# A Mamba-and-FFN sandwich block on one core: the chunk output computed turned, with the weights in the array and the decayed scores moving

## The reference, cut to what matters

```python
def step(state, inp):
    x_t, b_t, c_t, dt_t = inp
    decay = jnp.exp(dt_t * a)[..., None, None]
    b_bar = dt_t[..., None] * b_t
    state = decay * state + b_bar[..., None] * x_t[:, :, None, :]
    y_t = jnp.einsum('bhn,bhnp->bhp', c_t, state)
    return (state, y_t)
...
y = y + d_param[None, None, :, None] * xh
```

## Time and profile before

| | before |
|---|---|
| median of 3 runs | 1528.94 us (1528.52 to 1531.23) |
| the profiled execution: its time / its span | 1531.44 / 1529.7 us |
| PE (TensorE matmul) busy | 1426.4 us, 93% |
| PEld (weight loads) busy | 986.9 us, 65% |
| DVE (VectorE) / ACT (ScalarE) / POOL (GpSimd) busy | 1092.1 / 828.8 / 439.2 us |
| mean granted clock of TensorE | 0.974 |

### The profile page before, as it was taken

How to read it: one execution, slowest core, us unless ns; L and a number is a source line. 1 busy time by engine, 2 the same in 40 slices (tenths; PEclk the granted TensorE clock), 3 DMA queues, 4 the chain that set the end, 5 groups by cost and what they waited for, 6 DMA issues and landing times.

```text
span 1529.7 us, 28256 instructions
## 1 busy us (share of the span) xinstructions
PE 1426.4 (93%) x9712; PEld 986.9 (65%) x9712; DVE 1092.1 (71%) x2424; ACT 828.8 (54%) x1718; POOL 439.2 (29%) x487
## 2 busy tenths in 40 slices
PE   4999999998999989999999999999899999999776
PEld 3484758676485856758577675867658585675654
DVE  5454786858777686876859678685877769586665
ACT  3555574555745475553746447454674547555231
POOL 2020242214331232313422134321333134321343
PEclk8899999999999999999999999999999999999888
DMA  6000000101000010100001010010100000000000
GB/s 225 1 15 1 15 1 1 42 1 44 1 15 28 2 44 1 42 1 16 29 1 43 1 44 1 2 42 1 44 1 17 26 1 28 1 28 1 28 1 28
DMA packets 33351, 33.22 MB, mean 22 GB/s; under 512 B 4888, under 2 KB 31640, under 8 KB 33184
## 3 DMA queue, kind: packets, MB, share of 16 engines
q1 hardware_dynamic: 33184, 31.11, 6.2%
HBM read 22.72 MB, written 8.39 MB: 20 GB/s over the span
## 4 chain that ended last, share of the span: by engine, by line
PE 66%; issue 14%; DVE 10%; POOL 5%; ACT 2%; SPq 1%; DMA 0%; POOLq 0%; DVEq 0%; ACTq 0%
PE bank L1291 20%; PE bank L1473 7%; PE bank L1460 7%; PE bank L1377 6%; PE bank L1410 5%; PE bank L1445 4%; PE bank L1389 4%; PE bank L1369 3%; PE bank L1397 3%; PE bank L1359 2%; PE bank L1361 2%; SPq L548 1%; PE bank L1301 1%; DVE un L937 1%; POOL yT L670 1%
## 5 line engine op out<-in xcount | busy, mean ns | idle before, releaser
L686 POOL TENSOR_TENSOR xdw<-xdt,decays 128x512 f32<-128x512 f32 x64 | 66.7, 1043 | 430.3 <-DVE xdt L1043 408.1
L1291 PE MATMUL bank<-sh,WbT 128*128 128x512 f16 x768 | 174.3, 383 | 10.3 <-DVE sh L967 10.1
L1291 PE MATMUL bank<-sh,WcT 128*128 128x512 f16 x768 | 175.5, 379 | 0.0
L881 ACT ACTIVATE yk<-bank,decays 128x64 f32<-128x64 f32 x512 | 112.1, 330 | 86.4 <-PE bank L1389 86.4
L962 DVE SCALAR_TENSOR_TENSOR xs<-xi,taps,xs 128x512 f32<-128x512 f32 x192 | 152.5, 805 | 8.7 <-ACT xs L787 4.4
L1473 PE MATMUL bank<-sign2T,hh 128*128 128x256 f16 x1024 | 151.2, 275 | 2.0 <-DVE hh L1157 2.0
L868 ACT ACTIVATE mt<-bank 128x512 f32<-128x512 f32 x128 | 69.5, 596 | 148.3 <-PE bank L1361 148.3
L1410 PE MATMUL bank<-xdt,mt 128*128 128x64 f32 x1024 | 142.9, 262 | 0.0
L1291 PEld LDWEIGHTS bank<-sh,WbT 128*128 128x128 f16 x768 | 73.6, 98 | 100.6 <-issue 14.5
L1410 PEld LDWEIGHTS bank<-xdt,mt 128*128 128x128 f32 x1024 | 134.9, 192 | 2.2
L1291 PEld LDWEIGHTS bank<-sh,WcT 128*128 128x128 f16 x768 | 75.1, 98 | 87.1
(11 more groups left out here) (182 smaller groups left out, 2755.1 us busy)
## 6 DMA issues: line engine op xcount, KB each, us to landing
xt<-L_attn_input_tensor_dram SPq DMA_DIRECT2D x16, 512.0 KB, 4.8
u<-L_attn_input_tensor_dram SPq DMA_DIRECT2D x16, 512.0 KB, 3.7
out_dram<-u SPq DMA_DIRECT2D x16, 512.0 KB, 3.0
yT<-in_L_ffn_w_dram SPq DMA_DIRECT2D x2, 1024.0 KB, 14.1
zs<-in_L_attn_Wb_dram SPq DMA_DIRECT2D x1, 1024.0 KB, 8.6
zs<-in_L_attn_Wc_dram SPq DMA_DIRECT2D x1, 1024.0 KB, 10.8
BT<-in_L_attn_Wx_dram SPq DMA_DIRECT2D x1, 512.0 KB, 4.7
BT<-in_L_attn_Wz_dram SPq DMA_DIRECT2D x1, 512.0 KB, 6.1
```

Of the source, the lines that this page charges most:

```text
L686: pool.tensor_tensor(xdw[n % 2][:, :, :], xdt[n % 2][:, :, :], per_head(decays[:, 1, q, :]), ALU.mult)\
L881: last = nc.scalar.activation(yk[n % 2][:, h, :], bank(t, ("YI", j, q))[:, h * HD:(h + 1) * HD], ACT.Copy, scale=decays[:, 0, q, h:h + 1])
L1291: mm = nc.tensor.matmul(bank(t, key)[:, :], w[i][:, k, cols(m)], v[h][:, k, :], start=(a == 0), stop=(a == len(terms) - 1))
```

## The change

The output of a chunk is computed with channels on the partitions. `back` takes `xdt` (128 rows, 64 columns) as weights and moves `mt` (128 columns), and writes head h = 2c + g to partitions 64g to 64g + 63 and the columns of c. The part carried from the state goes into the same bank before it: `carry` takes the state as weights and moves `Cd`, which is C times the decay of each token. So Y needs neither yk nor a turn, and VectorE adds it to `yT` in one instruction. The step `turn` goes, with its keys and its place in all lists. YI is now the first part of Y, and a bank of Y is held from `carry` to the end of `back`.

`Cd` is new work: a product E in `front` (64 rows of fp16 weights, 512 columns moving), an Exp of 128x512 on ScalarE, and a multiplication of 128x512 by C on GpSimd. The decays lose their first third. `of_source` and `of_target` swap which of the two is kept by head group.

```diff
@@ PE front @@
-                    nc.tensor.matmul(bank(t, key)[:, :], of_source[:, q, :],
-                                     of_target[:, g].rearrange("p c t -> p (c t)"), start=False, stop=True)\
+                    nc.tensor.matmul(bank(t, key)[:, :], of_source[:, q, g, :],
+                                     of_target[:, :, :].rearrange("p c t -> p (c t)"), start=False, stop=True)\
                         .then_inc(full_sem(t, key), 1)
...
+                key = ("E", j, q)
+                pe.wait_ge(*empty(t, key))
+                nc.tensor.matmul(bank(t, key)[:, :], of_source[0:HALF, q].rearrange("p g s -> p (g s)")[:, HALF:HALF + P],
+                                 of_target[0:HALF, :, :].rearrange("p c t -> p (c t)"), start=True, stop=True)\
+                    .then_inc(full_sem(t, key), 1)
@@ PE carry @@
-                key = ("YI", j, q)
-                for need in latest(empty(t, key), st_out.count(t, n * HP) if n else st_zero.count(t, 1)):
+                key = ("Y", j, q)
+                for need in latest(empty(t, key), Cd_out.count(t, n + 1),
+                                   st_out.count(t, n * HP) if n else st_zero.count(t, 1)):
                     pe.wait_ge(*need)
                 for c in range(KI):
-                    mm = nc.tensor.matmul(bank(t, key)[:, cols(c)], CT[:, c, cols(q)], state[:, c, :],
-                                          start=True, stop=True)
-                mm.then_inc(full_sem(t, key), 1)
+                    mm = nc.tensor.matmul(bank(t, key)[:, cols(c)], state[:, c, :], Cd[r][:, c, :],
+                                          start=(c == 0), stop=False)
+                mm.then_inc(YI_done.sem, 1)
@@ PE back @@
-                for need in latest(empty(t, key), mt_out.count(t, (n + 1) * HP)):
-                    pe.wait_ge(*need)
+                pe.wait_ge(*mt_out.count(t, (n + 1) * HP))
                 for h in range(HEADS):
-                    mm = nc.tensor.matmul(bank(t, key)[:, h * HD:(h + 1) * HD], mt[r][:, h % HP, h // HP, :],
-                                          xdt[r][:, h, :], start=True, stop=True)
+                    c, g = h // HP, h % HP
+                    mm = nc.tensor.matmul(bank(t, key)[g * HD:(g + 1) * HD, cols(c)], xdt[r][:, h, :], mt[r][:, g, c, :],
+                                          start=False, stop=(h >= HEADS - HP))
@@ PE turn: the function goes @@
-                for c in range(KI):
-                    mm = nc.tensor.transpose(bank(t, key)[:, cols(c)],
-                                             yk[n % 2][:, HP * c:HP * c + HP, :].rearrange("p h n -> p (h n)"),
-                                             ident[:, :])
@@ PE sums @@
-                for n, w in enumerate((upto, after, ones)):
+                for n, w in enumerate((after, ones)):
@@ POOL front, after xdw @@
+                pool.wait_ge(*E_out.count(t, n + 1))
+                pool.wait_ge(*C_out.count(t, (j + 1) * KI))
+                pool.tensor_tensor(Cd[n % 2][:, :, :], Cd[n % 2][:, :, :], CT[:, :, q * P:(q + 1) * P], ALU.mult)\
+                    .then_inc(Cd_out.sem, 1)
@@ ACT front; ACT carry goes @@
-                for h in range(HEADS):
-                    last = nc.scalar.activation(yk[n % 2][:, h, :], bank(t, ("YI", j, q))[:, h * HD:(h + 1) * HD],
-                                                ACT.Copy, scale=decays[:, 0, q, h:h + 1])
+                act.wait_ge(*full(t, ("E", j, q)))
+                act.wait_ge(*YI_done.count(s, ch(sj, sq) + 1))
+                nc.scalar.activation(Cd[n % 2][:, :, :].rearrange("p c t -> p (c t)"), bank(t, ("E", j, q))[:, :],
+                                     ACT.Exp).then_inc(E_out.sem, 1)
@@ DVE back; DVE turn goes @@
-                nc.vector.tensor_tensor(yk[n % 2][:, :, :], yk[n % 2][:, :, :], heads(bank(t, ("Y", j, q))[:, :]),
-                                        ALU.add).then_inc(yk_out.sem, 1)
-                nc.vector.tensor_tensor(v, bank(t, ("YT", j, q))[:, :].rearrange("p (c t) -> p c t", c=KI), v,
+                nc.vector.tensor_tensor(v, bank(t, ("Y", j, q))[:, :].rearrange("p (c t) -> p c t", c=KI), v,
                                         ALU.add).then_inc(yT_out.sem, 1)
@@ turn_steps, second part of a block @@
-        steps += own(("turn", j, 0)) + [(who, "in_norm", nj)] + own(("front", j, 3)) + [(who, "xT", nj, 0)]
-        steps += tail(("end_stat", j)) + own(("carry", j, 2), ("back", j, 2), ("turn", j, 1)) + [(who, "xT", nj, 1)]
-        steps += tail(("end_root", j), ("end_norm", j)) + own(("carry", j, 3), ("turn", j, 2), ("back", j, 3))
+        steps += [(who, "in_norm", nj)] + own(("front", j, 3)) + [(who, "xT", nj, 0)]
+        steps += tail(("end_stat", j)) + own(("carry", j, 2), ("back", j, 2)) + [(who, "xT", nj, 1)]
+        steps += tail(("end_root", j), ("end_norm", j)) + own(("carry", j, 3), ("back", j, 3))
```

More of the change, by code:

```diff
@@ L290, in mamba_sandwich_kernel @@
         bt = [sb(f"bt{r}", [P, HEADS * NS]) for r in range(2)]
-        yk = [sb(f"yk{r}", [P, HEADS, HD]) for r in range(2)]
+        Cd = [sb(f"Cd{r}", [P, KI, P]) for r in range(2)]
         state = sb("state", [P, KI, P])
@@ L674, in front @@
                 if n == 0:
-                    pool.wait_ge(*full(t.ago(1), ("YI", NJ - 1, NQ - 1)))
+                    pool.wait_ge(*YI_done.count(t.ago(1), NCH))
                     pool.wait_ge(*st_out.count(t.ago(1), NCH * HP))
@@ L840, in project_c @@
                 s, sj = before_block(t, j)
-                for need in latest(full(t, ("C", j, c)), full(s, ("YI", sj, NQ - 1))):
+                for need in latest(full(t, ("C", j, c)), full(s, ("S", sj, NQ - 1, HP - 1))):
                     act.wait_ge(*need)
+                if c == 0:
+                    act.wait_ge(*Cd_out.count(s, (sj + 1) * NQ))
                 nc.scalar.activation(CT[:, c, :], bank(t, ("C", j, c))[:, :], ACT.Copy, scale=1.0 / (SW * SX))\
@@ L856, in decay_exp @@
                 act.wait_ge(*st_scaled.count(s, (sj + 1) * NQ))
-                act.wait_ge(*yk_part.count(s, (sj + 1) * NQ))
+                act.wait_ge(*xdw_out.count(s, (sj + 1) * NQ))
                 nc.scalar.activation(decays[:, :, :, :].rearrange("p a q h -> p (a q h)"),
-                                     bank(t, ("sums", j))[:, 0:3 * NQ * HEADS], ACT.Exp).then_inc(decays_out.sem, 1)
+                                     bank(t, ("sums", j))[:, 0:2 * NQ * HEADS], ACT.Exp).then_inc(decays_out.sem, 1)
             def front(t, j, q):
@@ L909, in _ @@
                 "z_in": gate_in, "z_silu": gate_silu, "silu": x_silu, "xs": x_high, "dt": step_exp,
-                "log": step_log, "cums": cum_top, "skip": skip_term, "C": project_c, "decays": decay_exp, "front": front, "carry": carry,
+                "log": step_log, "cums": cum_top, "skip": skip_term, "C": project_c, "decays": decay_exp, "front": front,
                 "gate": head_normalise, "uT": middle_high, "H": hidden})
@@ L1186, in _ @@
                 "dt": step_in, "log": step_mid, "decay": step_out, "B": project_b, "cums": decay_ends, "front": front,
-                "carry": carry, "back": back, "turn": turn, "head_stat": head_stats, "gn_sum": head_moments, "gn_root": head_variance,
+                "carry": carry, "back": back, "head_stat": head_stats, "gn_sum": head_moments, "gn_root": head_variance,
                 "gn_fold": head_fold, "gate": gate, "mid_stat": middle_stats, "mid_norm": middle_norm,
@@ L1191, in _ @@
             dve.wait_ge(masks_made, MASKS_MADE)
-            nc.vector.tensor_reduce(of_head[:, :], ident[:, :].rearrange("p (a h) -> p h a", h=HEADS), AX_X, ALU.add)\
-                .then_inc(picks, 1)
-            nc.vector.tensor_reduce(of_chunk[:, :], ident[:, :].rearrange("p (a q h) -> p q a h", q=NQ, h=HEADS), AX_XY,
+            nc.vector.tensor_reduce(of_pair[:, :], ident[:, :].rearrange("p (a c g) -> p c a g", c=KI, g=HP), AX_XY,
                                     ALU.add).then_inc(picks, 1)
+            for q in range(NQ):
+                nc.vector.tensor_reduce(of_chunk[:, q, :],
+                                        ident[:, :].rearrange("p (a q c g) -> p q g a c", q=NQ, c=KI, g=HP)[:, q], AX_XY,
+                                        ALU.add).then_inc(picks, 1)
             nc.vector.tensor_reduce(minus_low[:, :], ident[:, :].rearrange("p (a i n) -> p i a n", a=2, i=2)[:, 1], AX_XY,
@@ L1493, in _ @@
                 "xT": turn_input, "xi": project_x, "z": project_z, "dt": step_size, "B": project_b, "C": project_c,
-                "cums": running_sums, "sums": decay_sums, "front": front, "carry": carry, "back": back, "turn": turn, "gn_mean": head_means,
+                "cums": running_sums, "sums": decay_sums, "front": front, "carry": carry, "back": back, "gn_mean": head_means,
                 "Wo": attention_out, "uT": turn_middle, "H": hidden, "O": ffn_out,
```

90 lines of the change are left out of this document (36 added, 54 removed).

## The result

The changed kernel takes 1566.10 us, median of 4 runs (1565.82 to 1568.58); the kernel before takes 1530.03 us beside it (4 runs, 1528.52 to 1531.23). The ratio is 1.024, 95% interval 1.0222 to 1.0258: slower by 36 us. The forecast was 1568 us. The profiled execution took 1565.99 us with a span of 1564.2, so 34.5 us more span than before.

What follows compares the result with a forecast made beforehand. TensorE, busy 93% of the span, was taken as the bound. Terms of +68, -14, -16, +6, -3 and -2 gave +39 on 1531.4 us: 1570 profiled, 1568 as median; whole range 1506 to 1604.

Steps and rivals of the forecast that it cites:

- a border: On TensorE, a switch between whole-array and half-column products: 0.09 us plus one load that is not hidden.
- Rival B: Switching between whole and half columns costs nothing on TensorE: 0.43 us a head beside O, about 1507 us; chance 0.22.
- Rival D: Column switches cost nothing, but column halves don't run side by side: 1533 us; chance 0.08.
- C without overlap: Column switches each cost a bare load of 0.11 us, and halves don't run side by side: 1624 us; either variant 0.13.
- C with overlap: Column halves run side by side, but bare loads are 0.11 us at both switches: 1585 to 1605 us; either variant 0.13.
- back beside O: `back` interleaved with O in 28 chunks: 0.69 us a head instead of 0.39, adding 68 us.
- turns 0 and 3: The dropped turns in chunks 0 and 3 of each block: 32 times 0.44 us, saving 14 us.
- last stretch: A block's last two chunks, from xT's first half: 8.15 us instead of 9.11, saving 1.0 in each of 16 blocks.
- E: The new fp16 product behind S in `front`: 0.1 us, 64 times, adding 6 us.
- sums: A third of the sums product goes, two fp32 instructions of about 0.11 us, 16 times: saving 3 us.
- 4 backs alone: `back` without O in chunks 0 and 1 of the first batch: 0.48 us less each, saving 2 us.
- The step that failed: At a batch's end, VectorE's state addition comes 0.69 us earlier, so about 1.0 us of gain is kept.

Runs made afterwards that it cites:

- pairs: The changed kernel with two heads of `back`, then four products of O, instead of head by head: 1516.98 us, ratio 0.9914 to the kernel before.
- whole columns: The changed kernel with each head's `back` product taking its pair's 128 columns as weights, so outputs include the wrong head's part: 1511.43 us.
- halves apart: The changed kernel with all of `back` before O, and its four left-half heads before its four right-half heads: 1507.52 us.
- The loop written out: The changed kernel with the loop over batches 1 to 6 written out in every engine's program, without branches: 1556.14 us.
- back first: The changed kernel with all 8 heads of `back` run before the 32 products of O, instead of interleaved: 1496.45 us, ratio 0.9783 to the kernel before.
- the fastest kernel: The changed kernel with all of `back` before O and the loop over batches written out: 1483.48 us, ratio 0.969 to the kernel before.

## Why the prediction was right

The price that decided was right in its size and in its cause. "So a border costs 0.09 us plus one bare load" was read from the only border in the trace, one in rows, and it holds for columns: 0.69 us forecast, 0.69 measured, and the experiments with pairs and with whole columns take the number of borders and the shape away one at a time. Rival B (no border) gave 0.43 a head, which is what the run shows once the shape is whole. Rival D and C without overlap needed halves that don't run side by side, and pairs, halves apart and `back` alone rule that out; C with overlap needed a bare load of 0.11 at both borders, 0.84 a head where 0.69 is measured. How the 0.25 us divide between idle time and a bare load was not tested by itself, though the two parts of a head, 617.16 - 616.79 = 0.37 and 617.48 - 617.16 = 0.32 us, are the 0.365 and 0.325 of the forecast. The Trainium skill, "TensorEngine Tiling (Array Packing)", Key Properties, says that a change of tiling mode drains TensorE; this case's trace agrees, with idle time on the load queue at the changes of shape and 0.25 us for a head's two borders.

The terms, as forecast and as measured, in span:

| term | forecast | measured | how |
| --- | --- | --- | --- |
| back beside O, 28 times | +68 | +67 | 2.30 + 0.09 |
| turns 0 and 3 | -14 | -14 | 0.44 each |
| last stretch, 8 in the first block of a batch | -8 | -8 | 9.11 to 8.11 |
| last stretch, 8 in the second | -8 | -4 | 11.1 to 10.9 in five, 10.27 to 9.97 in one; about -2 in the last batch |
| E | +6 | 0 | S and E in S's 1.64 |
| sums | -3 | -3 | |
| 4 backs alone | -2 | -3 | 1.74 to 1.02 |
| half clock near the start of batches | none | -3 | 5 of them before, 3 after |
| together | +39 | +32 | the spans: +34.5 |

Of the 2.5 us that are left, 1 is the wait before S in the first chunk of each block, 0.26 us where it was 0.18; the rest is not placed.

That the total came within 2 us of the measured time is partly luck: the terms that were off happened to cancel in part. "I take 0.1" for E: it is nothing, as the last rows of S already run beside it. "8 x 0.11 plus a start of about 0.1, plus 0.15 to get in and 0.13 to get out: 1.26 us" for `back` alone: 1.02. It was worth little, since the wait before carry 3 took most of it in chunk 2. The half clock was left out of the sum.

The step that failed was at the end of a batch: "That addition comes earlier by the 0.69 us that VectorE saves, so 1.0 is about kept". It failed twice. First, the addition came only 0.3 us earlier: it ended 10.13 us into the stretch before (722.00 - 711.87) and 9.83 after (738.74 - 728.91). VectorE did save the 0.69 us, but the four instructions that normalise the end of the batch before, ahead of the addition, took longer:

```profile
718.64 2.59 DVE L937 TENSOR_SCALAR y<-y,moments_end,rstd_end 128x256 f32<-128x256 f32 x4
```

```profile
735.04 2.92 DVE L934 TENSOR_SCALAR y<-y,moments_end,rstd_end 128x256 f32<-128x256 f32 x4
```

Why they do stays open. Second, I read the 1.65 us of the earlier trace rows as a wait on VectorE because the row names VectorE as the releaser. Only 1.01 of it was, as the sixth pass shows; the rest was TensorE's branch, whose duration was in the trace before, in a view that I didn't ask for. After, the addition would have allowed a wait of 1.89 us, and the branch made it 2.55 to 2.92. So the 1.0 us forecast became 0.3 in the sixth pass, and anything from 0.4 won to 0.1 lost in the five others. The loop written out shows the branch's part once more: 1.89 us in every pass.

The busy times of the other engines went the way that was said. ScalarE fell by 76.7 us (forecast -112 + 38). VectorE fell by 33.1 where 44 were forecast; 8 of the missing 11 are two normalisations that took longer, y with 764 ns where it took 703 and xn with 618 where it took 549. GpSimd grew by 79 us instead of 67, as the multiplication that makes Cd takes 1.27 us and not xdw's 1.04, in the groups of instructions of after:

```profile
L689 POOL TENSOR_TENSOR Cd<-Cd,CT 128x512 f32<-128x512 f32 x64 | 81.3, 1271 | 46.8 <-ACT Cd L879 46.7
```

None of it held TensorE: no wait on Cd stands before a carry.

## What to carry to other kernels

Before two streams of products are interleaved, compare the part of the array that each uses. If they differ, every change over and back is a border (here 0.25 us for the pair), and a group behind a group costs one pair of them. The change itself was a good one. It lost 36 us by the order it was put in, and gains 33 us with `back` in one piece. Products in two halves of the array are best put alternately, next to each other in the queue.

An idle stretch of TensorE at the end of a loop's body may be its branch, whatever the row names as the releaser. It is hidden only by products issued before it, and a faster end of the body hides less. The last pass, where the loop ends, shows the same place with a short branch.

## What the runs showed of the hardware

- Halves of columns run side by side: 16 fp32 instructions that alternate between them in 1.02 us, 0.064 each, where the whole array takes 1.79 us. The Trainium skill, "TensorE: Matmul & The Clock Gate", Part 3, speaks of small products in different column groups that run concurrently. The trace of after agrees with 1.02 us.
- The overlap reached only what was near in the queue: with the halves eight instructions apart it was mostly lost (1.52 us).
- TensorE's branch back to the loop's start takes 3.3 to 3.7 us in these two kernels, and 0.08 us where the loop ends; that of ScalarE, GpSimd and VectorE takes 0.04 to 0.06 us.
- Behind the branch TensorE ran at the half clock (1.2 GHz) for a while in some batches and at the full one (2.4 GHz) in others, after idle times that hardly differ. In after, the same 24 products (timeline of TensorE; the batch with 5.35 us is shown above):

```profile
552.90 7.04 PE L1284 MATMUL bank<-xh,WxT 128*128 128x512 f16 x24 [2.79 <-issue]
```

The windows over them, granted clock third from last:

```profile
739.00:747.00 8.00, 7.08 (x35) 3.40 (x36) 5.59 (x20) 5.48 (x9) 1.16 (x2) 1.00 0.45 144
552.00:560.00 8.00, 7.10 (x27) 3.11 (x28) 4.25 (x15) 3.83 (x7) 0.34 (x1) 0.79 0.43 141
```

One such start costs 7.04 - 5.35 = 1.7 us. There were 5 in the loop of the kernel before (one of them 9 us into its batch), 3 in after, 4 with back first, 1 with halves apart and in the fastest kernel, none with whole columns. Why one batch gets it and the next doesn't stays open.
